# A routed layer's scatter queue: waiting for the block before only where the token ranges of the two blocks meet

## The reference

```python
# x: 8 x 256 x 256 = 2048 tokens of 256 features
def _L0_attn_ref(x, Wq, bq, Wk, bk, Wv, bv, Wo, bo):
    q, k, v = x @ Wq.T + bq, x @ Wk.T + bk, x @ Wv.T + bv
    phi_q, phi_k = elu(q) + 1.0, elu(k) + 1.0
    kv_sum = jnp.cumsum(phi_k * v, axis=1)
    context = (phi_q * kv_sum) * SCALE
    return context @ Wo.T + bo

def moe_forward(x, router_w, w1, w2, w_gate, w_up, w_down):   # E = 8, TOPK = 2, INTER = 512
    top_logits, top_indices = jax.lax.top_k(x @ router_w, TOPK)
    scores = jax.nn.softmax(top_logits, axis=-1)
    # each of a token's two experts: act = silu(g) * u with g, u = split(x @ w1[e]); act @ w2[e]
    combined = (unperm.reshape(T, TOPK, h) * scores[..., None]).sum(axis=1)
    shared = silu(x @ w_gate) * (x @ w_up) @ w_down
    return combined + shared

x = x + _L0_attn_ref(_layernorm(x), ...)
x = x + _L0_ffn_ref(_layernorm(x), ...)
```

## Time and profile before

| | |
|---|---|
| median of 3 runs | 391.1 us |
| the profiled execution's own time | 390.93 us |
| its span in the profile | 389.2 us |
| TensorE busy | 338.0 us, 87% |
| VectorE, ScalarE, GpSimd busy | 234.9, 214.0, 173.0 us |
| mean granted TensorE clock | 0.97 |
| indirect DMAs of the scatter | 40 (32 of line 730, 8 of line 725) |

### The profile page before, as it was taken

One profiled execution on the slowest core, in us unless ns is written; L12 is line 12 of the kernel. 1 busy time (PEld: TensorE's weight loads), 2 busy tenths in 40 slices (PEclk: granted clock), 3 DMA queues, 4 the chain that ended last, 5 costly groups with the idle time before them and its releaser, 6 DMA issues.

```text
span 389.2 us, 9009 instructions
## 1 busy us (share of the span) xinstructions
PE 338.0 (87%) x2867; PEld 252.5 (65%) x2867; DVE 234.9 (60%) x578; ACT 214.0 (55%) x385; POOL 173.0 (44%) x274
## 2 busy tenths in 40 slices
PE   6876499879899898996999899999999999999900
PEld 6755278768687787895988466556565656666600
DVE  5879967668696686975788554544544443443300
ACT  3768728668686686855536354554545455445400
POOL 4723275467684666435042224343334333344552
PEclk9989989999999999999999999999999999999965
DMA  6976142255572554726567349556556585477440
GB/s 193 373 176 195 27 112 76 64 115 186 133 218 61 131 177 103 194 81 166 171 218 151 94 72 109 85 79 92 90 89 103 70 109 86 76 97 96 52 43 5
DMA packets 77403, 46.41 MB, mean 119 GB/s; under 512 B 60976, under 2 KB 72496, under 8 KB 76976
## 3 DMA queue, kind: packets, MB, share of 16 engines
q1 hardware_dynamic: 63088, 35.08, 36.7%
q0 software_dynamic: 9600, 10.70, 17.8%
q10 hardware_dynamic: 4672, 0.07, 0.8%
HBM read 19.09 MB, written 12.97 MB: 82 GB/s over the span
## 4 chain that ended last, share of the span: by engine, by line
PE 45%; DVE 17%; POOL 10%; issue 9%; DMA 8%; ACT 6%; SPq 1%; POOLq 1%; DVEq 0%; ACTq 0%
PE bU L965 11%; PE bG L965 11%; PE bV L986 6%; PE bQ L986 5%; DMA out_y<-xs,dst_row 4%; PE bU L233 3%; DVE ab L1411 3%; DMA we<-in_w_shared 3%; POOL x_rows L567 2%; PE bK L945 2%; PE bG L233 2%; DVE al L1416 2%; DVE st L1288 2%; PE bD L233 1%; PE bT L233 1%
## 5 line engine op out<-in xcount | busy, mean ns | idle before, releaser
L730 POOL DMA_INDIRECT out_y<-xs,dst_row x32 | 50.6, 1581 | 75.3 <-issue 37.9
L1411 DVE SCALAR_TENSOR_TENSOR ab<-bU,sg 128x512 f32<-128x512 f32 x64 | 44.1, 689 | 65.0 <-PE bU L965 51.5
L1094 ACT ACTIVATE sg<-bG 128x512 f32<-128x512 f32 x64 | 37.8, 591 | 44.3 <-PE bG L965 26.7
L965 PE MATMUL bG<-we,work 128*128 (+1 forms) x216 | 52.7, 380 | 0.9 <-DVE wd L1467 0.9
L965 PE MATMUL bU<-we,work 128*128 (+1 forms) x216 | 52.6, 380 | 0.0
L567 POOL DMA_INDIRECT x_rows<-rows,slot_u x32 | 36.2, 1132 | 26.9 <-DVE slot_u L1462 10.5
L1238 ACT ACTIVATE ws_h<-ab 128x512 f16<-128x512 f32 x36 | 22.7, 630 | 41.5 <-DVE ab L1411 40.1
L1687 DVE TENSOR_TENSOR ws_h<-ab,ws_h 128x512 f16<-128x512 f32 x36 | 24.9, 693 | 20.7 <-ACT ws_h L1238 20.7
L1416 DVE TENSOR_TENSOR al<-ab,ah 128x512 f16<-128x512 f32 x32 | 22.1, 692 | 24.4 <-ACT ah L1101 24.3
L965 PEld LDWEIGHTS bG<-we,work 128*128 128x128 f16 (+1 forms) x216 | 20.8, 99 | 20.5 <-issue 2.9
L233 PE MATMUL bD<-ws_h,ah 128*128 128x256 f16 x112 | 21.4, 273 | 13.3 <-DVE al L1416 12.2
(11 more groups left out here) (289 smaller groups left out, 795.0 us busy)
## 6 DMA issues: line engine op xcount, KB each, us to landing
stage<-in_w_expert SPq DMA_DIRECT2D x24, 512.0 KB, 4.7
we<-in_w_shared SPq DMA_DIRECT2D x3, 1024.0 KB, 13.1
xs<-bo POOLq DMA_DIRECT2D x8, 256.0 KB, 3.9
out_y<-xs SPq DMA_DIRECT2D x8, 256.0 KB, 2.5
xs<-in_x SPq DMA_DIRECT2D x1, 1280.0 KB, 19.4
x_rows<-we SPq DMA_DIRECT2D x9, 134.0 KB
xs<-in_x SPq DMA_DIRECT2D x3, 256.0 KB, 4.1
work<-x_rows SPq DMA_TRANSPOSE x40, 3.1
```

The source lines that it names most:

```text
L730: pool.indirect_dma_start(out_rows, bass.IndirectOffsetOnAxis(ap=dst_row[:, b:b + 1], axis=0), ya[b % NY], None, bounds_check=NT * P - 1, ...
L965: ins = pe.matmul(dst[t * n:(t + 1) * n, :], x2[:, hi * KC + k, t * n:(t + 1) * n], w[t][lo][:, k, half, :], start=s == 0 and k == 0, stop ...
L1094: act.activation(sg[q][:], src[:], ACT.Silu, scale=1.0 / WS).then_inc(S["sg_done"], 1)
L1411: dve.scalar_tensor_tensor(out=ab[q][:], in0=src[:], scalar=1.0 / WS, in1=sg[q][:], op0=ALU.mult, op1=ALU.mult).then_inc(S["a_done"], 1)
```

## The change

Two more indirect DMAs by GpSimd gather from `x_rows` the token numbers of the first and of the last row of each slot. They are put into the form of the plan, spread over the partitions by a second small matmul (`spread_ends`, issued by TensorE after block 1's `expert_up`), copied out by VectorE behind block 1's `routed_act_lo`, and compared by GpSimd: a block is held for the block before only where the expert number rises and the token ranges of the two meet. A last block that is not full counts as reaching to token 2048. All blocks from 3 on read their count, the mixed ones and those behind them too (these from partition 64). The second half of a mixed block now waits for the block before as well as for the first half.

```diff
+            for t in range(2):
+                then(pool.tensor_scalar(tok_at[:, t:t + 1], row_at[:], P * RW / 2.0, ends_at[:, t + 1:t + 2], ALU.mult, ALU.add), wait=t == 1)
             ...
             pool.wait_ge(S["padded"], 16 * (E + 1))
             pool.nop(nofuse=True)
+            for t in range(2):
+                pool.indirect_dma_start(tok_id[:, t:t + 1], None, words, bass.IndirectOffsetOnAxis(ap=tok_at[:, t:t + 1], axis=0)
+                                        ).then_inc(S[f"tok_in{t}"], 16)
             for b in range(NX):
                 pool.reg_load(meta_reg, blk_row[b:b + 1, :])
                 ...
+            pool.wait_ge(S["spread_in"], 2)
+            then(pool.tensor_scalar(tok_f[:, 2:3], rows_of[:, 0:1], ends_at[:, 0:1], None, ALU.is_ge), wait=False)
+            for t in range(2):
+                pool.wait_ge(S[f"tok_in{t}"], 16)
+            then(pool.tensor_copy(tok_f[:, 0:2], tok_id[:]))
+            pool.tensor_scalar(ends[:, 0, :], pick_block[:], tok_f[:, 0:1], None, ALU.mult).then_inc(S["ends_in"], 1)
+            then(pool.tensor_scalar(tok_f[:, 3:4], tok_f[:, 1:2], float(NT * P), tok_f[:, 2:3], ALU.subtract, ALU.mult))
+            then(pool.tensor_scalar(tok_f[:, 1:2], tok_f[:, 3:4], float(NT * P), None, ALU.add))
+            pool.tensor_scalar(ends[:, 1, :], pick_block[:], tok_f[:, 1:2], None, ALU.mult).then_inc(S["ends_in"], 1)
             pool.wait_ge(S["spread_out"], 2)
             ...
+            pool.wait_ge(S["ends_out"], 1)
+            then(pool.tensor_tensor(above[:, 1:NBLK], first_tok[:, 1:NBLK], last_tok[:, 0:NBLK - 1], ALU.subtract), wait=False)
+            then(pool.tensor_tensor(below[:, 1:NBLK], first_tok[:, 0:NBLK - 1], last_tok[:, 1:NBLK], ALU.subtract))
+            then(pool.tensor_scalar(above[:, 1:NBLK], above[:, 1:NBLK], 0.0, None, ALU.is_le), wait=False)
+            then(pool.tensor_scalar(below[:, 1:NBLK], below[:, 1:NBLK], 0.0, None, ALU.is_le))
+            then(pool.tensor_tensor(above[:, 1:NBLK], above[:, 1:NBLK], below[:, 1:NBLK], ALU.mult))
+            then(pool.tensor_tensor(pad_f[:, 1:NBLK], pad_f[:, 1:NBLK], above[:, 1:NBLK], ALU.mult))
             ...
             def held(b):
-                return 3 <= b < NBLK and b not in MIXED and b - 1 not in MIXED
+                return 3 <= b < NBLK

             def load_hold(b):
-                pool.reg_load(hold_reg[b % 2], hold_i[0:1, b:b + 1])
+                row = HALF if b - 1 in MIXED else 0
+                pool.reg_load(hold_reg[b % 2], hold_i[row:row + 1, b:b + 1])
             ...
                         if t == 1:
+                            pool.wait_ge(before, 16 * ((b + 1) // 2))
                             pool.wait_ge(S["halves_out"], 16 * (q + 1))
             ...
+            def spread_ends():
+                pe.wait_ge(S["ends_in"], 2)
+                pe.wait_ge(S["spread_out"], 2)
+                pe.matmul(bR[:, 0:2 * NBLK], spread_w[:], ends[:].rearrange("p s b -> p (s b)"), start=True, stop=True
+                          ).then_inc(S["ends_ps"], 1)
             ...
+                if b == 1:
+                    dve.wait_ge(S["ends_ps"], 1)
+                    dve.tensor_copy(both_toks, bR[:, 0:2 * NBLK].rearrange("p (s b) -> p s b", s=2)).then_inc(S["ends_out"], 1)
```

More of the change, by code:

```diff
@@ L52, in layer_kernel @@
     MIXED = [MIX0 + GAP * q for q in range(NPAIR)]
-    N_CONST = 32
+    N_CONST = 35
     BIG = 2 * NT * P
@@ L191, in layer_kernel @@
         meta = plan[:, 5 * NBP:9 * NBP].bitcast(U16).rearrange("p (b n) -> p b n", n=8)
+        ends_at = sb("ends_at", [P, 4])
+        tok_at, tok_id, tok_f = sb("tok_at", [P, 2], U32), sb("tok_id", [P, 2], I32), sb("tok_f", [P, 4])
+        ends = plan[:, 9 * NBP:10 * NBP].bitcast(F16)[:, 0:2 * NBLK].rearrange("p (s b) -> p s b", s=2)
+        first_tok, last_tok = (plan[:, n * NBP:n * NBP + NBLK] for n in (10, 11))
+        both_toks = plan[:, 10 * NBP:12 * NBP].rearrange("p (s b) -> p s b", s=2)[:, :, 0:NBLK]
+        above, below = (plan[:, n * NBP:n * NBP + NBLK] for n in (12, 13))
         meta_tok = meta[:, :, 0:2].bitcast(I32)
@@ L195, in layer_kernel @@
         dst_row = sb("dst_row", [P, NBP], I32)
-        hold0, hold_i = (sb(n, [P, NBP], I32) for n in ("hold0", "hold_i"))
+        hold0, hold_i = sb("hold0", [P, NBP], I32), plan[:, 14 * NBP:15 * NBP].bitcast(I32)
         end_i = sb("end_i", [P, E], I32)
@@ L218, in layer_kernel @@
             tok_done tanh_done t_done rows_clear saved0 saved1
-            rt pt slot_const spread_in spread_ps spread_out end_done padded bexp_done pad_done
+            rt pt slot_const spread_in spread_ps spread_out ends_in ends_ps ends_out tok_in0 tok_in1 end_done padded bexp_done pad_done
             xg_in0 xg_in1 xg_in2 xg_in3 first_meta0 first_meta1 first_meta2 first_meta3 meta_in0 meta_in1 meta_in2 meta_in3 sign_done score_done dst_done ta_ps ath_done atl_in0 atl_in1 atl_in2 o_ps y_done hold_done row_done lent tl_ps atl_last halves_out scattered0 scattered1""".split()
@@ L615, in slot_constants @@
                     const(pool.tensor_tensor(at_slot[:, 2:3], at_slot[:, 0:1], at_slot[:, 3:4], ALU.mult), wait=True)
+                    const(pool.tensor_scalar(ends_at[:, 0:1], at_slot[:, 0:1], -0.5, 1.0, ALU.mult, ALU.add))
+                    const(pool.memset(ends_at[:, 1:2], float(D)))
+                    const(pool.tensor_scalar(ends_at[:, 2:3], at_slot[:, 0:1], -HALF * RW / 2.0, D + (P - 1) * RW / 2.0, ALU.mult, ALU.add))
                     const(pool.tensor_scalar(spread_w[:, 0:HALF], ones16[:, 0:HALF], at_slot[:, 3:4], None, ALU.mult))
@@ L674, in _ @@
             meta_reg = pool.alloc_register("meta_reg")
+            words = xrows.rearrange("r c -> (r c)").bitcast(I32).rearrange("(r o) -> r o", o=1)
             pool.wait_ge(S["row_done"], 1)
+            pool.wait_ge(S["slot_const"], N_CONST)
+            for t in range(2):
+                then(pool.tensor_scalar(tok_at[:, t:t + 1], row_at[:], P * RW / 2.0, ends_at[:, t + 1:t + 2], ALU.mult, ALU.add), wait=t == 1)
             for i in (B - 2, B - 1):
@@ L1010, in _ @@
                     expert_down(b - 2)
+                if b == 1:
+                    spread_ends()
                 if b < NBLK - 1:
```

## The result

The changed kernel takes **380.97 us** (median of 4 runs, 380.52 to 381.99); beside it the kernel before took 391.33 (4 runs, 389.35 to 392.77). The ratio is 0.9742, with a 95% interval of 0.9695 to 0.979. The profiled execution took 381.11 us, with a span of 379.5. The forecast was 381.7, and 379.8 for the span.

What follows compares the result with a forecast made beforehand. The end was taken as set by GpSimd's scatter queue running behind the results. Span 389.2 − 9.8 + 0.2 + 0.2 = 379.8 us, 381.5 with the 1.7 around it, forecast 381.7 as run median; range 379.3 to 385.0.

Steps and rivals of the forecast that it cites:

- both sorts of wait: GpSimd's scatter queue: waits for the block before at expert changes (6 removed) and at mixed blocks (8 removed).
- the three terms given for it: Block 35's scatter starts at the latest of result (370.7), issue (371.3) and block 33's landing and 1.0 (371.6).
- (c): The gathers' 256 small packets meet the last weight load: 0.2 us taken, from 0 to 1.
- (d): Second small matmul in TensorE's full stretch: 0.2 us taken.
- The fixed end: Span ends 7.8 us after the last scatter's start; bounds: drain follows the landing, or 1 us of it does not.
- (a): Three constants on GpSimd in the first stage, 0.2 to 0.3 us each: 0 taken, at most 0.8.
- (e): Hold values later on GpSimd: first scatters may start up to 1 us later; 0 taken.
- (f): Count loads at all blocks on GpSimd: 8 more, 0.3 us, already within the 1.5 after a landing; 0 taken.
- (b): Two GpSimd gathers ahead of the meta loads: 2.6 to 2.9 us, covered; 0 taken, from 0 to 2 us.
- rival of the late start: Gathers or VectorE's waits delay the second stage by 2 to 4 us, giving 384 to 386 us; chance 0.05.
- No effect: All waits stay, through meeting ranges or values read from the wrong slot: 391.5 us; chance 0.03.
- slower gather: GpSimd waits for late gathered words, holding up VectorE and TensorE; 394 us if landing takes 20 us; chance 0.03.

Runs made afterwards that it cites:

- the first three experiments: Changed kernel with waits for the block before kept only at expert changes, 380.91 us; only at mixed blocks, 380.92 us; at both, 390.72 us.
- the first two experiments: Changed kernel with waits for the block before kept only at expert changes, 380.91 us; then only at mixed blocks and those behind them, 380.92 us.
- the eight gathers: Changed kernel with each of its two gathers issued four times, the copies going to an unread tile: 388.28 us.
- the experiment without gathers: Kernel before with its waits for the block before removed from block 3 on, except mixed second halves, without the added work: 380.88 us.
- four gathers: Changed kernel with each of its two gathers issued twice, the copies going to an unread tile: 381.81 us.

## Why the prediction was right

- **The bound and the backlog.** Right. TensorE was busy for 138.38 of 139 us, and the whole gain lies behind 355. That the backlog takes both sorts of wait, which the prediction wrote under its rivals ("the queue comes level before the end in either case"), is shown by the first three experiments: 380.91, 380.92, and 390.72 with both.
- **The last start.** 371.6 was predicted, 371.52 measured; 9.86 us gained, 9.8 predicted. What stands behind it is the issue of block 34, 369.67 + 1.85 = 371.52, one of the three terms given for it; the landing of block 33 would have allowed it at about the same time (in the first two experiments block 35 stands 1.88 and 1.92 behind block 34 and not 1.85). Block 22 was to be under 4 us late and was 3.3; the second half of block 5 starts 4.69 behind the first, 4.7 predicted.
- **The sum.** The span was to be 379.8 and is 379.5. The last start moved by 9.86 with all that is added already in it, where the sum took 9.8 off and put 0.4 on for (c) and (d); the end behind it grew by 0.16. The other 0.4 us of the forecast's error are the spread of the runs: the profiled execution stands 0.14 over their median, and 0.2 under it was assumed.
- **The sign was stated too widely.** Scatters of blocks 21 to 35 were to start 0.85 behind their results. Blocks 21 and 22 are 3.3 late and 23 is 1.0 late, as the same prediction's own sum had it (3.1, 2.7, then level by 23); 24 to 34 are at 0.85, and 35 is at 1.39.
- **The fixed end.** 7.8 us behind the last start was an assumption on one observation. It was 7.98 after, and 7.75 to 8.4 in all the others, 7.8 also where the last scatter was a full block. Of the two bounds that were given, neither showed.
- **(a), (c), (d), (e), (f), small terms.** No run shows a price for any of them. The first routed products start at 216.09 where they started at 215.91, but this place lies between 215.13 and 217.14 in the twelve traces of all kernels but that of the eight gathers, and at 216.28 in the experiment without gathers, so the 0.18 is no measure of (c). The second small product took 0.20, as in (d), but the next product starts 0.03 behind its start, and the first result stands 11.01 us behind the first routed product, 11.00 before: the 0.2 of (d) did not come. The first scatter starts 1.00 behind its result, 0.98 before, so (e) is nothing. (a) and (f) can't be seen. Results were 0.24 to 0.28 late in this one pair of traces, 0.18 of it from the stage's start.
- **(b), the gathers, right in price and wrong in three of its steps.** The price was 0, and VectorE's idle time of 0.67 shows it. But the words land 5.8 us after issue, at 213.9, and are needed at 213.1: "they land before they are needed" did not hold, and 0.92 us was waited. Two of the six small operations took 1.42 and 1.32 us instead of 0.3. And the pads came at 216.90, not at 215.0 to 216.0. The 1.0 us of cover on GpSimd was used up, and what kept the price at 0 was the 1.27 us on VectorE behind it, of which 0.6 went. That the price was still 0 is in part luck, as three steps were wrong and the reserve on VectorE took them. The rival of the late start was nearer than it was thought: with the cover used up, six more gathers cost 6.5 us.
- **The Trainium skill's fit.** By the Trainium skill, "DMA: Bandwidth & Descriptors", section "Anatomy of one DMA — SWDGE (gpsimd) path", a landing is an estimated 2.3 us, by which a change of expert would have cost nothing. The landing is 3.9 us at the median, and in the kernel before the last three changes of expert alone were worth 5.75 us; the measurement decides against the page here.
- **The other rivals.** "No effect" and "slower gather" did not come: a gather of 128 words lands in 5.8 us, 0.3 under the longest landing of the earlier trace rows, and the experiment with both sorts of wait kept shows what "no effect" would have looked like.

## What to carry to other kernels

A queue that runs behind its producer is priced by its backlog at the end, not by its number of waits: compare the rhythm of the queue with that of the results in each mode, and find the block at which it comes level. A wait that is caught up later costs nothing, the same wait at the last step costs all of itself, and of two causes, here, either could be removed alone for the full gain. The gain belongs to inputs like these: where the token ranges of neighbouring blocks meet, the waits come back, and with all of them back the kernel takes as long as before. Work that is added ahead of a stage has to be laid against the cover of every engine behind it, as what is over may cost more than its length: with eight gathers TensorE's clock fell behind the idle time.

## What the runs showed of the hardware

- **GpSimd's end follows the issue of its last scatter.** The span ends 7.75 to 8.4 us behind the last scatter's start in all twelve traces behind the one of the earlier trace rows, with a full block last (7.8) as with an empty one (7.8 in the kernel before), and with the last two DMAs 1.85 or 3.51 us apart.
- **Small operations of GpSimd are slow beside VectorE's large conversions.** The 128x1 operations of lines 703 and 708 take 0.32 to 0.35 us by themselves, but 1.24 to 1.96 when they run beside a conversion of 128x1024 from f32 to f16. Line 708 stands beside the last one in seven of the traces, at 1.24 to 1.34 us; with the gathers doubled or more it is behind it, at 0.32 and 0.33, and with four gathers another, the cast of 128x2, stands there and takes 1.01 instead of 0.19. Line 703 starts 0.06 to 0.13 us ahead of a conversion in five traces and takes 1.38 to 1.96; in two it starts 0.16 and 0.22 ahead and takes 0.32. In the changed kernel the two slow ones end just behind the conversion beside them: 211.67 + 1.42 = 213.09 against 211.80 + 1.22 = 213.02, and 214.80 + 1.32 = 216.12 against 214.70 + 1.23 = 215.93. That they wait for it there is inferred from these times; no run isolates it.
- **A gather of 128 words of 4 bytes can land as late as a large scatter**: 5.8 us for both in the changed kernel, against 2.7 to 6.1 for the scatters. In the other traces with two gathers the slower one takes 5.5 to 5.9, and in three of them the faster one only 2.9 to 3.2. The meta loads behind took longer as well: 4.3 to 5.2 us, where they took 1.9 to 4.7 before.
- **TensorE's clock fell behind one idle time of 4 us.** With eight gathers it stood idle for 3.95 us, and the granted clock was 0.62 over the 4.5 us behind that and 1.00 from there on. That is 1.7 us of work, of which 1.3 reached the results. It is one trace.
